# Two unread products of 512 columns ahead of the first transposes of the probabilities in layers 1 and 3

## The chip, the cores and the metric

The kernel runs on one core of one Trainium2 chip. Times are device microseconds of that core. The median of three runs before the change is 2001.88 us (1987.11 to 2002.51). One execution was also profiled: it took 1999.9 us, of which the program's instructions span 1998.0 us.

## The reference

128 boards of 64 squares with 256 features pass through four layers. Each layer adds to x a function of h = relu(layernorm(x)). Layers 0, 1 and 3 are masked attention (8, 4 and 4 heads), layer 2 is a gated graph layer with tanh scores.

```python
def _L1_gnn_ref(x, adjacency_mask, Wq, Wk, Wv, Wo, bo):
    q = split_heads(x @ Wq)
    k = split_heads(x @ Wk)
    v = split_heads(x @ Wv)
    sim = jnp.einsum('bhid,bhjd->bhij', q, k) * scale
    sim = jnp.where(adjacency_mask[:, None, :, :], sim, neg)
    attn = jax.nn.softmax(sim, axis=-1)
    out = jnp.einsum('bhij,bhjd->bhid', attn, v)
    return out @ Wo + bo
...
h = jnp.maximum(_layernorm(x, axis=-1), 0.0)
x = x + _L1_gnn_ref(h, adj, L1_gnn_Wq, ...)
```

Layer 3 is the same function as layer 1 with weights of its own.

## The kernel before

Four boards (256 tokens) make a group, and there are 32 groups. Two groups are worked on at a time, in two slots with buffers and semaphores of their own; 16 passes take all groups. Slot 1 runs half a pass behind slot 0: each engine goes through the same list of steps (`STEPS`) for both slots, merged by a table of numbers (`ORDER`), so on every engine the order of the two slots' steps is fixed and written out. PE's program is unrolled over all 16 passes. Engines meet only through semaphores.

An attention step list for one slot on PE is: `turn` (transposes of the normalised x, L609), `q`, `k`, `v` (the projections, each weight split into a high and a low part of type fp32r), `scores`, then for each half of the heads `pt` (transposes of the probabilities, L683), `heads` (probabilities times v), and at the end `out` (the output projection, tile oT). Every product goes through the helper `mm`, so PE's rows name L483 whatever the step; the tiles tell the steps apart: `kT,qT` is `scores`, `probsT,v` is `heads`, `w_hi,oT` and `w_lo,oT` are `out`, and `consts,probs` are the transposes of `pt`.

Around `pt` the steps hand work to and fro. DVE masks the scores (L1164), takes the row maximum (L1170), ACT takes the exponential (L914), DVE normalises (L1178, L1180). PE's `pt` waits for that (`probs`). ACT copies the transposed probabilities to SBUF (L921), `heads` waits for the copy, ACT and DVE split the result into high and low parts (L924, L989, tile oT), and `out` waits for both parts.

With the lag between the slots, layer 1 of one slot always runs beside layer 3 of the other. So there are two kinds of stretch in a pass. In what is called stretch A here, slot 1 is in layer 1 and slot 0 in layer 3; in stretch B it is the other way round. In A, PE's order is: `v` of layer 3, `pt` 0 of layer 1, `scores` of layer 3, `heads` 0, `pt` 1 and `heads` 1 of layer 1, `out` 0 of layer 1, `pt` 0 of layer 3, `out` 1 of layer 1, `heads` 0, `pt` 1, `heads` 1 and `out` 0 of layer 3, and then layer 2 of slot 1 begins. In B, `pt` 0 of layer 1 stands between the two halves of `v` of layer 3, `scores` of layer 3 stands ahead of the last `heads` of layer 1, and both `out` of layer 1 stand ahead of `pt` 0 of layer 3.

PSUM has four banks of 512 columns for each slot. Bank 3 holds v until ACT has copied it out (`v_sb`, L906); the next steps that write it are `heads` 0 and, later, `out` 1.

Of the kernel before, what the change touches and what calls it, by code (L numbers as in the profile page):

```python
# [29 lines left out]
P = 128  # L30
# [126 lines left out]
def build(nc, x_in, adjq_in, adjt_in, mats_in, cols_in, rows_in, cst_in, out):  # L157
# [8 lines left out]
    with ctx:  # L166
        def sb(name, shape, dt, scope=ctx):
            return scope.enter_context(nc.sbuf_tensor(name, shape, dt))
# [9 lines left out]
        WHI = sb("w_hi", [P, MATS, DC, D], F32R)  # L178
# [91 lines left out]
        def bank(s, n):  # L270
            return PS[:, 4 * s + n, :]
# [42 lines left out]
        def units(a):  # L314


            first, blocks = ((0, 2), (4, 1), (6, 1))[a]
            return [(first + 2 * j + cj, 2 * j + cj, j, cj) for j in range(blocks) for cj in range(2)]

        def turned(a):  # L320

            us = units(a)
            return [us[0:2], us[2:4]] if len(us) == 4 else [us[0:1], us[1:2]]

        def norm_halves(a, v):

            return v.eight[2 * NORM_OF[a]:2 * NORM_OF[a] + 2]
# [56 lines left out]
        def alone(eng):  # L384


            eng.sem_inc(setup["waited"], 1)
# [93 lines left out]
        def _(pe):  # L481
            def mm(o, lhsT, rhs, start, stop):
                return nc.tensor.matmul(o, lhsT, rhs, start=start, stop=stop, skip_group_check=True)  # L483
# [121 lines left out]
            def transposed_h(s, a, t, v):  # L605

                pe.wait_ge(S[s]["xn_ready"], norm_halves(a, v)[t])
                for c in range(DC):
                    last = nc.tensor.transpose(bank(s, H_BANKS[c])[:, t * P:t * P + P],  # L609
                                               XN[s][:, t * D + c * P:t * D + c * P + P], IDENT)  # L610
                    if t == TT - 1:
                        last.then_inc(S[s]["hT_ps"], 1)

            def features_out(s, o, m, oc, halves=None):


                for c in range(DC):
                    if halves:
                        pe.wait_ge(S[s]["hT_hi"], halves[c])
                    mm(o, WHI[:, m, c, oc * P:oc * P + P], HT[s][:, 0, c, :], c == 0, False)  # L620
                    mm(o, WLO[:, m, c, oc * P:oc * P + P], HT[s][:, 0, c, :], False, False)
                for c in range(DC):
                    if halves:
                        pe.wait_ge(S[s]["hT_lo"], halves[c])
                    last = mm(o, WHI[:, m, c, oc * P:oc * P + P], HT[s][:, 1, c, :], False, c == DC - 1)
                return last

            def tokens_out(o, actT, t, m, start=True, ready=(), halves=()):

                at = slice(t * P, t * P + P)
                for c in range(DC):
                    if ready and t == 0:
                        pe.wait_ge(ready[0], halves[c])
                    mm(o, actT(0, c)[:, at], WHI[:, m, c, :], start and c == 0, False)
                    mm(o, actT(0, c)[:, at], WLO[:, m, c, :], False, False)
                for c in range(DC):
                    if ready and t == 0:
                        pe.wait_ge(ready[1], halves[c])  # L640
                    last = mm(o, actT(1, c)[:, at], WHI[:, m, c, :], False, c == DC - 1)
                return last

            def att(s, k, a, i, v):
                sm, L, n = S[s], ATT[a], v.att[a]
                hd = D // L["heads"]
                two = L["heads"] == 8
                if k == "turn":
                    transposed_h(s, a, i, v)
                elif k in ("q", "k"):  # L650
                    b = 1 if k == "q" else 2
                    last = features_out(s, bank(s, b)[:, i * TOK:i * TOK + TOK], L["mats"] + b - 1, i,
                                        norm_halves(a, v) if k == "q" and i == 0 else None)
                    if i == DC - 1:
                        last.then_inc(sm[k + "_ps"], 1)
                elif k == "v":
                    last = tokens_out(bank(s, 3)[:, i * D:i * D + D], lambda j, c: HT[s][:, j, c, :], i, L["mats"] + 2)
                    if i == TT - 1:
                        last.then_inc(sm["v_ps"], 1)
                elif k == "scores":  # L660

                    pe.wait_ge(sm["q_sb"], n)
                    pe.wait_ge(sm["k_sb"], n)
                    alone(pe)
                    if two:

                        pe.wait_ge(sm["v_sb"], n)
                        alone(pe)
                    for b in range(NB):
                        for u, m, _, _ in units(a):  # L670
                            for half, h in enumerate(HEADS_AT[a][m]):
                                r, c = h * hd % P, h * hd // P
                                last = mm(bank(s, m)[SQ * half:SQ * half + SQ, b * SQ:b * SQ + SQ],
                                          Q[s][r:r + hd, c, b * SQ:b * SQ + SQ],
                                          K[s][r:r + hd, c, b * SQ:b * SQ + SQ], True, True)
                            if b == NB - 1:
                                last.then_inc(sm["s_ps"], 1)
                elif k == "pt":

                    for u, _, j, cj in turned(a)[i]:  # L680
                        pe.wait_ge(sm["probs"], v.eight[u])
                        for at in range(cj * TOK, cj * TOK + TOK, P):
                            last = nc.tensor.transpose(bank(s, 1 - i)[:, at:at + P], PR[s][:, j, at:at + P], IDENT)  # L683
                    last.then_inc(sm["pt_ps"], 1)
                elif k == "heads":

                    pe.wait_ge(sm["v_sb"], n)
                    pe.wait_ge(sm["pt_sb"], v.six[2 * a + i])
                    alone(pe)
                    place = {h: (m, half) for m, pair in enumerate(HEADS_AT[a]) for half, h in enumerate(pair)}  # L690
                    for t in range(TT):
                        for h in range(i * L["heads"] // 2, (i + 1) * L["heads"] // 2):
                            m, half = place[h]
                            _, _, j, cj = units(a)[m]
                            r, at = h * hd % P, cj * 256 + t * P + half * SQ
                            for e in range(2):
                                last = mm(bank(s, O_BANKS[i] + e)[r:r + hd, t * SQ:t * SQ + SQ],
                                          V[s][SQ * e:SQ * e + SQ, t, h * hd:h * hd + hd],
                                          PTS[s][SQ * e:SQ * e + SQ, j, at:at + SQ], True, True)
                    last.then_inc(sm["o_ps"], 1)  # L700
                elif k == "out":
                    if i == 0:

                        pe.wait_ge(sm["oT_lo"], v.six[2 * a])
                    tokens_out(bank(s, Y_BANKS[i])[:, 0:D], lambda j, c: OT[s][:, j, c, :], i, L["mats"] + 3,
                               ready=(sm["oT_hi"], sm["oT_lo"]), halves=v.six[2 * a:]).then_inc(sm["y_ps"], 1)
# [106 lines left out]
            def step(s, what, v):  # L813
                k, a, i = what
                if a == L2:
                    l2(s, k, i, v)
                else:
                    att(s, k, a, i, v)
# [481 lines left out]
```

## Time and profile before

| what | before |
|---|---|
| median of the runs | 2001.88 us |
| profiled execution | 1999.9 us |
| its span | 1998.0 us |
| PE busy | 1842.2 us, 92% |
| DVE busy | 1381.1 us, 69% |
| ACT busy | 996.2 us, 50% |
| granted PE clock, mean | 0.966 |

The first rows of the table are times, the others are from the first part of the page. Busy is the union of an engine's instructions; the rest of the span the engine waits or issues. The granted clock is 1.00 at 2.4 GHz and 0.50 at 1.2 GHz, so its mean over a stretch tells which share of that stretch ran at the lower level.

### The profile page before, as it was taken

The page shows a single profiled execution, that of the slowest core. Times are in us where ns is not written, and L with a number is a line of the kernel's source. Part 1 is how long each engine was busy: PE and PEld are TensorE (multiplying, and loading weights), DVE is VectorE, ACT ScalarE, POOL GpSimd, SP SyncE. Part 2 cuts the span into 40 slices and gives each one's busy share as a digit, 9 for nine tenths or more (in the row PEclk, how much of TensorE's full clock was granted, in tenths as well). Part 3 has the DMA queues.
Part 4 walks back from the last instruction along what each step waited for, and adds up shares of the span by engine and source line. Part 5 has one row for each costly group of instructions (what it writes and reads, how often), then busy time and mean ns, then how long its engine had stood idle before and what let it go on. Part 6 is the DMA issues. An engine that isn't in the chain of part 4 may idle for free.

```text
span 1998.0 us, 58204 instructions
## 1 busy us (share of the span) xinstructions
PE 1842.2 (92%) x23623; PEld 1637.1 (82%) x23623; DVE 1381.1 (69%) x3777; ACT 996.2 (50%) x3707; POOL 153.1 (8%) x265
## 2 busy tenths in 40 slices
PE   7999999999999999999999999999999999999997
PEld 6787888887888887888888888888888888888886
DVE  4677677777677776667677667677677766767674
ACT  4545455445455545455445455445455545455452
POOL 0000000000000000000000000000000000000000
PEclk8999999999999999999999999999999989999898
DMA  6000000000000000000000000000000000000000
GB/s 196 1 13 8 13 13 8 12 13 8 13 13 8 12 13 8 13 13 8 12 13 8 13 13 8 12 13 8 13 13 8 11 13 8 13 13 8 12 7 6
DMA packets 36564, 30.62 MB, mean 15 GB/s; under 512 B 11600, under 2 KB 36176, under 8 KB 36368
## 3 DMA queue, kind: packets, MB, share of 16 engines
q1 hardware_dynamic: 36368, 27.48, 4.6%
q8 instruction: 187, 3.06, 0.6%
q14 instruction: 9, 0.07, 0.0%
HBM read 19.08 MB, written 8.39 MB: 14 GB/s over the span
## 4 chain that ended last, share of the span: by engine, by line
PE 75%; DVE 16%; ACT 4%; issue 4%; DMA 0%; DVEq 0%; SPq 0%; POOL 0%; POOLq 0%
PE ps L483 68%; PE ps L609 3%; PE ps L683 3%; DVE small L1091 2%; ACT probs L914 2%; DVE f L1250 1%; DVE f L1248 1%; DVE xn L1103 1%; DVE x L1255 1%; DVE oT L989 1%; DVE small L1097 1%; DVE kT L1150 1%; DVE probs L1164 1%; PE ps L806 1%; DVE probs L1180 1%
## 5 line engine op out<-in xcount | busy, mean ns | idle before, releaser
L483 PE MATMUL ps<-hT,w_hi 128*128 128x256 f32 x2560 | 487.7, 284 | 3.1 <-DVE hT L1117 1.4
L483 PE MATMUL ps<-w_hi,hT 128*128 128x256 f32 (+1 forms) x1536 | 423.8, 344 | 0.0
L483 PEld LDWEIGHTS ps<-hT,w_hi 128*128 128x128 f32 x2560 | 406.7, 190 | 6.7 <-DVE hT L1117 1.8
L914 ACT ACTIVATE probs<-probs,small 128x64 f32<-128x64 f32 x1024 | 342.1, 337 | 93.7 <-DVE small L1170 92.0
L483 PE MATMUL ps<-hT,w_lo 128*128 128x256 f32 x1280 | 332.8, 282 | 0.0
L483 PEld LDWEIGHTS ps<-w_hi,hT 128*128 128x128 f32 x1536 | 267.6, 188 | 42.6 <-DVE wh L1222 11.5
L470 POOL TENSOR_TENSOR small<-small,consts 128x1 f32<-128x1 f32 x256 | 151.1, 590 | 1818.6 <-DVE small L1099 1818.6
L483 PE MATMUL ps<-w_hi,oT 128*128 128x256 f32 x768 | 207.7, 335 | 56.4 <-DVE oT L989 47.5
L483 PE MATMUL ps<-w_lo,hT 128*128 128x256 f32 (+1 forms) x768 | 249.5, 337 | 0.0
L483 PEld LDWEIGHTS ps<-hT,w_lo 128*128 128x128 f32 x1280 | 243.7, 190 | 0.0
L483 PEld LDWEIGHTS ps<-w_hi,oT 128*128 128x128 f32 x768 | 150.0, 215 | 75.3 <-DVE oT L989 64.2
L914 ACT ACTIVATION_READ_ACCUMULATOR probs<-probs,small 128x1 f32 x1024 | 194.2, 190 | 0.0
L889 ACT ACTIVATE hT<-ps 128x256 fp32r<-128x256 f32 x256 | 86.1, 382 | 209.5 <-PE ps L609 209.5
L921 ACT ACTIVATE probsT<-ps 128x256 f32<-128x256 f32 (+1 forms) x192 | 87.7, 457 | 153.4 <-PE ps L683 149.9
L483 PEld LDWEIGHTS ps<-w_lo,hT 128*128 128x128 f32 x768 | 144.6, 188 | 10.7
L483 PE MATMUL ps<-probsT,v 64*64 64x64 f32 (+1 forms) x4096 | 95.7, 235 | 40.7 <-issue 40.7
L1190 DVE TENSOR_TENSOR x<-ps,x 128x256 f32<-128x256 f32 x192 | 81.3, 424 | 74.6 <-PE ps L483 74.3
L1117 DVE SCALAR_TENSOR_TENSOR hT<-ps,hT 128x256 fp32r<-128x256 f32 x256 | 98.0, 419 | 50.1 <-ACT hT L889 48.2
L483 PE MATMUL ps<-w_hi,ct_hi 128*128 128x256 f32 x512 | 127.0, 286 | 4.0 <-DVE ct_lo L1234 2.9
L483 PEld LDWEIGHTS ps<-probsT,v 64*64 64x64 f32 (+1 forms) x4096 | 68.4, 127 | 70.2 <-issue 60.4
L483 PE MATMUL ps<-w_lo,ct_hi 128*128 128x256 f32 x512 | 124.2, 281 | 0.9 <-issue 0.9
L609 PE MATMUL ps<-consts,xn 128*128 128x128 f32 x512 | 94.0, 299 | 31.9 <-DVE xn L1103 31.7
(128 smaller groups left out, 3330.5 us busy)
## 6 DMA issues: line engine op xcount, KB each, us to landing
x_next<-x SPq DMA_DIRECT2D x32, 256.0 KB, 2.6
out<-x SPq DMA_DIRECT2D x32, 256.0 KB, 2.2
raw_lo<-mats SPq DMA_DIRECT2D x6, 1024.0 KB, 10.0
adj<-adjq SPq DMA_DIRECT2D x64, 16.0 KB, 2.0
raw_hi<-mats SPq DMA_DIRECT2D x1, 1024.0 KB, 11.5
adjT<-adjt SPq DMA_DIRECT2D x64, 8.0 KB, 2.3
raw_lo<-mats SPq DMA_DIRECT2D x1, 512.0 KB, 8.2
raw_consts<-board_consts SPq DMA_DIRECT2D x1, 451.5 KB, 3.0
```

Of the source, the lines that this page charges most:

```text
L470: nc.gpsimd.tensor_tensor(RSTD[s][:, i:i + 1], VE[s][:, i:i + 1], HALF, ALU.pow).then_inc(sm["rstd"], 1)
L483: return nc.tensor.matmul(o, lhsT, rhs, start=start, stop=stop, skip_group_check=True)
L609: last = nc.tensor.transpose(bank(s, H_BANKS[c])[:, t * P:t * P + P], XN[s][:, t * D + c * P:t * D + c * P + P], IDENT)
L683: last = nc.tensor.transpose(bank(s, 1 - i)[:, at:at + P], PR[s][:, j, at:at + P], IDENT)
L806: last = nc.tensor.transpose(bank(s, HAT_BANKS[i])[:, t * P:t * P + P], F[s][:, t * D + i * P:t * D + i * P + P], IDENT)
L889: fn(HT[s][:, 0, c, :], bank(s, H_BANKS[c])[:, 0:TOK], ACT.Relu).then_inc(S[s]["hT_hi"], 1)
L914: last = fn(p, p, ACT.Exp, bias=ROWMAX[s][:, row:row + 1], accum_out=ROWSUM[s][:, row:row + 1])
L921: fn(PTS[s][:, j, at], bank(s, 1 - i)[:, at], ACT.Copy).then_inc(sm["pt_sb"], 1)
L989: return tt(o, full, hi.bitcast(F32), ALU.subtract)
L1091: nc.vector.bn_stats(STATS[s][:, t, :], (XP if a == 0 else X)[s][:, t * D:t * D + D]).then_inc(S[s]["bn"], 1)
L1117: stt(HT[s][:, 1, c, :], bank(s, H_BANKS[c])[:, 0:TOK], 0.0, HT[s][:, 0, c, :].bitcast(F32), ALU.max, ALU.subtract).then_inc(S[s]["hT_lo"], 1)
L1190: tt(X[s][:, at], bank(s, Y_BANKS[i])[:, 0:D], X[s][:, at], ALU.add).then_inc(sm["res"], 1)
```

## The change

Ahead of the first transposes of the probabilities (`pt` with i = 0) in layers 1 and 3, PE now waits for `v_sb` and then multiplies a part of the weights by weights, 128 by 128 by 512 columns, twice, into bank 3 of the slot. Nobody reads the result. The steps of the other engines stay as they are. That adds 2 products in each of 2 layers, 2 slots and 16 passes, 64 pairs or 128 products in all.

```diff
                 elif k == "pt":
 
+                    if a > 0 and i == 0:
+
+                        pe.wait_ge(sm["v_sb"], n)
+                        alone(pe)
+                        for _ in range(2):
+                            mm(bank(s, 3), WHI[:, 0, 0, 0:P], WHI[:, 0, :, :].rearrange("p c o -> p (c o)"), True, True)
                     for u, _, j, cj in turned(a)[i]:
                         pe.wait_ge(sm["probs"], v.eight[u])
```

On PE in stretch A of the first pass, the first pair comes in like this (w_hi are weights, hT is h transposed, the number behind a semaphore is the slot):

```order
 L483 MATMUL ps<-w_lo,hT 128x256
 L483 MATMUL ps<-w_hi,hT 128x256 x2
-L683 MATMUL ps<-consts,probs 128x128 [waits probs_1]
-L683 MATMUL ps<-consts,probs 128x128
+L483 MATMUL ps<-w_hi 128x512 [waits v_sb_1]
+L483 MATMUL ps<-w_hi 128x512
+L689 MATMUL ps<-consts,probs 128x128 [waits probs_1]
+L689 MATMUL ps<-consts,probs 128x128
 L483 MATMUL ps<-kT,qT 64x64 [waits q_sb_0,k_sb_0]
 L483 MATMUL ps<-kT,qT 64x64 x15
```

The pair stands between `v` of slot 0 and the transposes of slot 1; the transposes, and the scores of slot 0 behind them, stand two products later.

On PE in stretch A, the second pair comes in behind the first `out` of slot 1:

```order
 L483 MATMUL ps<-w_lo,oT 128x256
 L483 MATMUL ps<-w_hi,oT 128x256 [waits oT_lo_1] x2
-L683 MATMUL ps<-consts,probs 128x128 [waits probs_0]
-L683 MATMUL ps<-consts,probs 128x128
+L483 MATMUL ps<-w_hi 128x512 [waits v_sb_0]
+L483 MATMUL ps<-w_hi 128x512
+L689 MATMUL ps<-consts,probs 128x128 [waits probs_0]
+L689 MATMUL ps<-consts,probs 128x128
 L483 MATMUL ps<-w_hi,oT 128x256
 L483 MATMUL ps<-w_lo,oT 128x256
```

The second `out` of slot 1 moves back with the transposes of slot 0.

On PE in stretch B, the second pair comes in behind both `out` of slot 0:

```order
 L483 MATMUL ps<-w_lo,oT 128x256
 L483 MATMUL ps<-w_hi,oT 128x256 x2
-L683 MATMUL ps<-consts,probs 128x128 [waits probs_1]
-L683 MATMUL ps<-consts,probs 128x128
+L483 MATMUL ps<-w_hi 128x512 [waits v_sb_1]
+L483 MATMUL ps<-w_hi 128x512
+L689 MATMUL ps<-consts,probs 128x128 [waits probs_1]
+L689 MATMUL ps<-consts,probs 128x128
 L483 MATMUL ps<-probsT,v 64x64 [waits v_sb_1,pt_sb_1]
 L483 MATMUL ps<-probsT,v 64x64 x7
```

Here `heads` of slot 1 is next, and moves back too. The transposes are the old ones; their line is L689 in the changed kernel.

## Rows read from the trace of the kernel before

**Rows 1.** Page, parts 1 and 4: busy time, chain that ended last
```profile
PE 1842.2 (92%) x23623; PEld 1637.1 (82%) x23623; DVE 1381.1 (69%) x3777; ACT 996.2 (50%) x3707; POOL 153.1 (8%) x265
...
PE 75%; DVE 16%; ACT 4%; issue 4%; DMA 0%; DVEq 0%; SPq 0%; POOL 0%; POOLq 0%
```

**Rows 2.** Busy time and granted clock (PEclk) of the middle and of single stretches
```profile
core 0: us, PE busy (x) PEld busy (x) DVE busy (x) ACT busy (x) POOL busy (x), PEclk, DMA share, GB/s
125.00:1970.00 1845.00, 1721.41 (x22422) 1532.04 (x22415) 1297.06 (x3568) 932.74 (x3517) 142.73 (x242) 0.97 0.04 11
...
608.80:623.80 15.00, 12.07 (x157) 10.51 (x156) 11.47 (x37) 8.56 (x35) 1.99 (x4) 0.89 0.05 19
...
728.00:743.00 15.00, 12.07 (x167) 10.22 (x165) 12.17 (x40) 8.59 (x35) 2.40 (x4) 1.00 0.06 19
...
910.00:925.00 15.00, 12.28 (x153) 10.53 (x153) 10.70 (x35) 8.63 (x33) 1.44 (x3) 0.77 0.02 5
```

**Rows 3.** Waits of PE: who waited for whom
```profile
engine line waited for: us in total, times, longest us
PE ps L483 <- DVE oT L989: 47.5, 71, 1.3
PE ps L483 <- issue: 41.6, 77, 1.0
...
PE ps L683 <- DVE probs L1180: 3.1, 1, 3.1
```

**Rows 4.** Timeline of PE, stretch A, full clock (start, length, instruction, count, idle before)
```profile
728.32 0.38 PE L683 MATMUL ps<-consts,probs 128*128 128x128 f32 x2
...
731.41 0.39 PE L483 MATMUL ps<-w_hi,oT 128*128 128x256 f32 x1 [0.38 <-DVE oT L989]
...
733.35 0.38 PE L683 MATMUL ps<-consts,probs 128*128 128x128 f32 x2
...
737.11 0.38 PE L483 MATMUL ps<-w_hi,oT 128*128 128x256 f32 x1 [0.93 <-DVE oT L989]
...
743.55 0.36 PE L483 MATMUL ps<-hT,w_hi 128*128 128x256 f32 x1
```

**Rows 5.** Timeline of PE, another stretch A, in which the clock falls
```profile
609.10 0.38 PE L683 MATMUL ps<-consts,probs 128*128 128x128 f32 x2
...
614.12 0.38 PE L683 MATMUL ps<-consts,probs 128*128 128x128 f32 x2
...
625.25 0.36 PE L483 MATMUL ps<-hT,w_hi 128*128 128x256 f32 x1
```

**Rows 6.** Timeline of PE, a stretch B at full clock
```profile
668.56 0.38 PE L683 MATMUL ps<-consts,probs 128*128 128x128 f32 x2
...
684.61 0.36 PE L483 MATMUL ps<-hT,w_hi 128*128 128x256 f32 x1
```

**Rows 7.** Timeline of PE, another stretch B, in which the clock falls
```profile
909.62 0.38 PE L683 MATMUL ps<-consts,probs 128*128 128x128 f32 x2
...
913.71 0.39 PE L483 MATMUL ps<-w_hi,oT 128*128 128x256 f32 x1 [1.27 <-DVE oT L989]
...
915.97 0.63 PE L683 MATMUL ps<-consts,probs 128*128 128x128 f32 x2
...
920.03 0.41 PE L483 MATMUL ps<-w_lo,oT 128*128 128x256 f32 x1
920.24 0.50 PE L483 MATMUL ps<-w_hi,oT 128*128 128x256 f32 x1
...
927.49 0.36 PE L483 MATMUL ps<-hT,w_hi 128*128 128x256 f32 x1
```

**Rows 8.** Timeline of PE: products of 512 columns in layer 2, full clock
```profile
579.58 0.63 PE L483 MATMUL ps<-w_hi,hT 128*128 128x512 f32 x2
580.05 0.40 PE L483 MATMUL ps<-w_lo,hT 128*128 128x512 f32 x1
```

**Rows 9.** Timeline of DVE in the stretch B of Rows 7
```profile
912.12 0.42 DVE L1164 SCALAR_TENSOR_TENSOR probs<-ps,mask_adj 128x256 f32<-128x256 f32 x1 [1.36 <-PE ps L483]
```

## The prediction

> **What bounds the kernel now.** I read the busy times first, then the chain of work that ended last. PE is busy 92% of the span and carries 75% of the chain; DVE has 16%, ACT 4% [rows 1]. So work added to PE costs its full time, unless it falls into a wait. The next view is the list of PE's waits [rows 3]. The reader should look for the place where the pairs go in. The transposes of the probabilities (L683) waited for the softmax once in the whole run, 3.1 us, and that is the last one, at the end of the last pass. At the other 63 places PE comes straight from its previous product. The waits lie elsewhere: in front of `out`, for the split result of `heads` (47.5 us in 71 waits for DVE's oT), and in front of `heads` ("issue", 41.6 us in 77 waits).
>
> Then I read the granted clock. From 125 to 1970 us it is 0.97 on average [rows 2], so 0.03 / 0.5 x 1845 = 111 us run at 1.2 GHz. Cut into stretches of 15 us around A and B, of which 31 can be laid, the clock is 1.00 in ten, 0.89 in thirteen, 0.77 in five and about 0.67 in three; [rows 2] has one of each of the first three kinds. That is 13 x 3.4 + 5 x 6.8 + 3 x 10.2 = 109 us, so nearly all of the half-clock time of the loop lies in A and B, the two places where one slot's layer 1 runs beside the other's layer 3.
>
> **What half clock costs.** The same work is measured at both levels. In A, from the first transposes of layer 1 to the same product of layer 2 takes 743.55 - 728.32 = 15.23 us at full clock [rows 4] and 625.25 - 609.10 = 16.15 us where 3.4 us are at half [rows 5]: 0.92 us more. In B it is 684.61 - 668.56 = 16.05 us [rows 6] against 927.49 - 909.62 = 17.87 us with 6.8 us at half [rows 7]: 1.82 us more. Both are 0.27 us for each microsecond at half clock, since PE waits for much of such a stretch. All 109 to 111 us cost about 30 us. That is the most that this change can give back through the clock.
>
> **What the change adds.** It adds 64 pairs of products of 512 columns, and nothing to another engine. No trace of before has such a product at these places, but layer 2 has the same form: two of them take 580.05 - 579.58 = 0.47 us of PE at full clock [rows 8]. At half clock a product of 256 columns takes 920.24 - 920.03 = 0.21 us [rows 7], so a pair takes 4 x 0.21 = 0.84 us there. From below the bound is nothing, if the pair lies wholly in a wait. I take 0.47, the row of the same form at the clock at which most pairs run: the transposes behind the second pair take 0.38 us in [rows 4] and [rows 5], and 0.63 us in [rows 7] at half clock; 12 of the 63 places are of the latter kind, all of them second pairs.
>
> The added wait for `v_sb` costs nothing. ACT copies v before it takes the exponentials of the same unit, and these stand ahead of the probabilities that the transposes wait for. What would be queued behind it, if it were late, is all of PE.
>
> Now whether a pair lies beside other work. **First pair**: PE goes from `v` to the transposes with no wait [rows 4 to 7], so the transposes start 0.47 us later, and with them the scores of the other slot and `heads`. DVE cannot use the time: in B it stands 1.36 us waiting for just those scores [rows 9]. ACT's copy of the transposes, the masks, the exponentials and the split of oT all follow from the two, so the wait in front of `out` (0.38 us in A, 1.27 us in B) does not shrink but moves back. **Second pair**: it follows `out` with no wait either, and delays transposes, ACT's copy, `heads`, oT and the next `out`. In A the wait of 0.93 us in front of that `out` moves back too, except for a tenth or so that DVE had in hand. After the stretch PE is dense again in layer 2 and has no slack to make the delay good.
>
> Sum: 63 x 0.47 = 29.6 us, and the last pair is free, since PE waits 3.1 us there [rows 3]. The profiled execution took 1999.9 us, 2.0 us under the median of the runs. 1999.9 + 29.6 = 2029.5, so I forecast **2030 us**. At half clock a pair fills time that other work would have spent at half clock, and so I add nothing for the 12 such places; the upper bound is 12 x (0.84 - 0.47) = 4.4 us more.
>
> **What the pairs do to the clock.** In [rows 5] the second pair's place, 614.12, still has transposes of 0.38 us, and the fall comes later, when `heads` and the wait in front of the last `out` have passed. In [rows 7] the clock has fallen by 915.97, after the wait of 1.27 us in front of `out`, and the second pair's place is just behind it. So in neither stretch does a pair stand in the wait that precedes the fall. It stands 2 to 4 us ahead of it, or behind it. A pair makes PE's work denser where it already came without a gap, and leaves the waits as long as they are. I take the half-clock time as unchanged.
>
> The Trainium skill speaks on this: "TensorE: Matmul & The Clock Gate", section "Why this matters for your kernels", asks for no idle gaps of PE over some 3 us between bursts of matmuls. By that rule there is nothing to win here, for no wait of the loop is that long. The trace does not agree that shorter waits are harmless: the longest in front of `out` is 1.3 us [rows 3], and the clock falls behind it [rows 7]. So by the rule the sum stays 2030 us, and by the trace up to 30 us could come back, which makes the first rival.
>
> **The rivals.**
> 1. The pairs hold the clock up. For it: they add work to the very stretches in which it falls, and ten of 31 stretches stay at 1.00 as it is, so the margin is small. Against it: the waits stay. If all half-clock time goes, the time is 2029.5 - 30 = 1999.5 us; if half goes, 2014.5 us. I give 0.22, and the two ends are its range: no change that can be measured.
> 2. The other side: the pairs are swallowed by waits behind them, because DVE, not PE, sets when `out` starts, and the clock is held as well. It decides at the wait in front of `out`: if that shrinks by 0.47 us, the 31 first pairs cost nothing, 14.6 us, and the 16 second pairs of A, in front of a wait of 0.93 us, another 7.5 us. With the clock gain the time is 2029.5 - 14.6 - 7.5 - 30 = 1977 us. DVE's wait for PE [rows 9] speaks against it. I give 0.05.
> 3. More half-clock time. The pairs lengthen the thin stretches, and waits and falls shift against each other. If all ten stretches that are now at 1.00 fell as the others do, this would add 10 x 0.92 to 10 x 1.82, that is 9 to 18 us: 2039 to 2048 us. I give 0.13.
>
> **How the numbers follow.** The forecast has 0.60: 2030 us, with 2020 to 2036 as its own range, from pairs that are in part absorbed and from the 4.4 us at half clock. The range for 8 in 10 leaves out the second rival, the outer third of the first and the far end of the third: 2004 to 2042 us. A measurement of this kernel tells about 1% from no change, here 1982 to 2022 us. Faster than that is the second rival, 0.05. Within it lie the first rival and a small part of the forecast, 0.25. Slower has 0.70.
>
> **What would show it.** In the profile after, a pair should take 0.47 us at full clock, straight behind `v` or `out` and with no wait ahead, and the waits of PE for oT should add up to about the same 47 us. Should these fall by 15 us or more, the second rival holds. The mean granted clock should stay at 0.97 between 125 and 1970 us; at 0.99 or 1.00 the first rival holds, at 0.95 the third. A full-clock stretch A, from the transposes of layer 1 to the product of layer 2, should be 15.23 + 0.47 = 15.7 us, as the first pair lies ahead of its start. What would make the forecast wrong is, above all, how near the stretches are to holding their clock, which the trace of before does not tell.

## The result, and the profile after

| what | before | after |
|---|---|---|
| median of the runs, us | 1998.34 (four runs) | 2028.36 (2020.53 to 2031.36, four runs) |
| ratio after / before | | 1.0153, 95% interval 1.0100 to 1.0207 |
| profiled execution, us | 1999.9 | 2020.53 |
| its span, us | 1998.0 | 2018.6 |
| its mean granted clock | 0.966 | 0.976 |

The change makes the kernel 1.5% slower, 30 us. Of the four executions after, the profiled one is the fastest; the other three took 2026.98, 2029.73 and 2031.36 us at mean granted clocks of 0.970, 0.968 and 0.967.

The first part of the page after:

```profile
PE 1861.8 (92%) x23751; PEld 1646.0 (82%) x23751; DVE 1380.5 (68%) x3777; ACT 997.0 (49%) x3707; POOL 152.1 (8%) x265
...
PE 75%; DVE 15%; ACT 4%; issue 4%; DMA 0%; DVEq 0%; SPq 0%; POOL 0%; POOLq 0%
```

Against [rows 1] PE has 128 instructions and 19.6 us more, and nearly nothing else has moved: PE is still 92% busy and still carries 75% of the chain.

The timeline of PE after, in a stretch A at full clock (start, length, instruction, count, idle before), answers to [rows 4]; w_hi alone, 128x512, is a pair:

```profile
619.47 0.62 PE L483 MATMUL ps<-w_hi 128*128 128x512 f32 x2
619.93 0.38 PE L689 MATMUL ps<-consts,probs 128*128 128x128 f32 x2
...
623.02 0.38 PE L483 MATMUL ps<-w_hi,oT 128*128 128x256 f32 x1 [0.38 <-DVE oT L995]
...
624.95 0.63 PE L483 MATMUL ps<-w_hi 128*128 128x512 f32 x2
625.41 0.38 PE L689 MATMUL ps<-consts,probs 128*128 128x128 f32 x2
...
629.18 0.39 PE L483 MATMUL ps<-w_hi,oT 128*128 128x256 f32 x1 [0.93 <-DVE oT L995]
...
635.59 0.36 PE L483 MATMUL ps<-hT,w_hi 128*128 128x256 f32 x1
```

The reader should see three things. A pair takes 619.93 - 619.47 = 0.46 us, and neither pair has a wait ahead of it. The waits of 0.38 and 0.93 us in front of `out` are as long as before. And the stretch takes 635.59 - 619.93 = 15.66 us against 15.23 us, 0.43 us more for the one pair that lies between these two rows. The list of PE's waits (us in total, times, longest) agrees:

```profile
PE ps L483 <- DVE oT L995: 48.2, 78, 1.3
PE ps L483 <- issue: 44.2, 78, 1.3
...
PE ps L689 <- DVE probs L1186: 2.3, 1, 2.3
```

In [rows 3] these were 47.5, 41.6 and 3.1 us: nothing was swallowed, but for 0.8 us at the very last place. The clock of the profiled execution is another matter. Busy times and granted clock of the loop, of two stretches A and, in the last row, of a stretch B:

```profile
core 0: us, PE busy (x) PEld busy (x) DVE busy (x) ACT busy (x) POOL busy (x), PEclk, DMA share, GB/s
125.00:1970.00 1845.00, 1717.99 (x22284) 1521.40 (x22284) 1286.29 (x3548) 928.27 (x3503) 141.72 (x242) 0.98 0.04 11
619.00:634.00 15.00, 12.06 (x163) 10.03 (x162) 11.36 (x37) 8.73 (x37) 1.83 (x4) 1.00 0.06 19
...
1349.00:1364.00 15.00, 12.30 (x153) 9.96 (x152) 10.62 (x33) 8.11 (x33) 1.49 (x3) 0.89 0.02 5
1043.80:1058.80 15.00, 12.06 (x156) 10.54 (x155) 10.80 (x34) 8.58 (x32) 1.65 (x3) 0.89 0.05 17
```

The loop has 0.98 where it had 0.97 [rows 2]. This view rounds the clock to two digits; the clock records of the two traces, added up over the loop, hold 68 us at half clock in place of 109. In the second stretch A shown (from 1349 us), 3.4 us run at half clock, and its two rows in the timeline are these:

```profile
1349.32 0.38 PE L689 MATMUL ps<-consts,probs 128*128 128x128 f32 x2
...
1366.25 0.36 PE L483 MATMUL ps<-hT,w_hi 128*128 128x256 f32 x1
```

It takes 16.93 us, 1.27 us more than at full clock. Before, the same 3.4 us cost 0.92 us [rows 4, 5]. One stretch against one says little, so here are all thirty stretches that lie whole in the loop, by the clock records and the timelines. Each is timed from the first projection of layer 3 to the first product behind the turn of the next group, and its cost is what it takes beyond the median of its kind that kept the clock:

| | before | after, profiled execution |
|---|---|---|
| A: kept its clock; at half for 3.4 us; for 6.8 us | 4; 11; none | 6; 7; 2 |
| B: kept its clock; at half for 3.4 us; 6.8 us; 10.2 us | 6; 1; 5; 3 | 8; 6; none; 1 |
| half-clock time in A and in B, us | 37.5 and 68.3 | 37.5 and 30.7 |
| what it cost in all, us | 30.3 | 23.9 |
| cost of a microsecond at half clock, us | 0.29 (0.24 to 0.35) | 0.35 (0.27 to 0.44) |

The half-clock time went in B, where the second pair stands just behind the wait after which the clock falls; the last row of busy times is such a stretch, with 0.89 where [rows 2] has 0.77. But each microsecond at half clock cost more. This is one execution of each kernel; no trace shows the others.

### The profile page after: what moved, and what is told of

Same layout as the page of the kernel before. It is cut to its first block, busy times and chain, and to the rows that moved or that the text cites. A ratio compares the mean times of both kernels' runs of the same rounds, so it can differ in the third digit from the quotient of the medians.

```text
span 2018.6 us, 58524 instructions
## 1 busy us (share of the span) xinstructions
PE 1861.8 (92%) x23751; PEld 1646.0 (82%) x23751; DVE 1380.5 (68%) x3777; ACT 997.0 (49%) x3707; POOL 152.1 (8%) x265
## 3 DMA queue, kind: packets, MB, share of 16 engines
HBM read 19.08 MB, written 8.39 MB: 14 GB/s over the span
## 4 chain that ended last, share of the span: by engine, by line
PE 75%; DVE 15%; ACT 4%; issue 4%; DMA 0%; DVEq 0%; SPq 0%; POOL 0%; POOLq 0%
PE ps L483 68%; PE ps L689 3%; PE ps L609 3%; DVE small L1097 2%; ACT probs L920 2%; DVE f L1256 1%; DVE xn L1109 1%; DVE oT L995 1%; DVE f L1254 1%; DVE x L1261 1%; DVE kT L1156 1%; DVE small L1103 1%; ACT probsT L927 1%; DVE probs L1170 1%; PE ps L812 1%
## 5 line engine op out<-in xcount | busy, mean ns | idle before, releaser
L483 PE MATMUL ps<-w_hi,oT 128*128 128x256 f32 x768 | 201.4, 326 | 57.5 <-DVE oT L995 48.2
L483 PEld LDWEIGHTS ps<-w_hi,oT 128*128 128x128 f32 x768 | 144.7, 207 | 76.9 <-DVE oT L995 65.4
```

## The experiments

Two theories were to be told apart. The first: the pairs lie on PE's path and cost their length, and the clock falls because of the waits, in which no pair stands. The second: what counts for the clock is how much work there is in a stretch, wherever it stands, so the pairs do hold it up, and there are only too few of them. The runs of before that went with these kernels have a median of 1995.96 us with the first four (granted clock 0.965 to 0.973) and 1995.76 us with the others (0.957 to 0.973).

| run | products per pass, place | median, us | ratio, 95% interval | granted clock of its runs |
|---|---|---|---|---|
| the change | 8, ahead of `pt` | 2028.36 | 1.0153 (1.0100 to 1.0207) | 0.967 to 0.976 |
| e1_first | 4, ahead of `pt`, layer 1 | 2024.67 | 1.0132 (1.0079 to 1.0185) | 0.952 to 0.969 |
| e2_second | 4, ahead of `pt`, layer 3 | 2018.95 | 1.0122 (1.0094 to 1.0150) | 0.961 to 0.972 |
| e3_four | 16, ahead of `pt` | 2066.57 | 1.0347 (1.0327 to 1.0367) | 0.965 to 0.969 |
| e4_fill | 12, in the waits ahead of `out` | 1970.83 | 0.9865 (0.9845 to 0.9886) | 0.992 to 0.993 |
| e5_moved | 8, in the waits ahead of `out` | 1972.93 | 0.9891 (0.9857 to 0.9926) | 0.988 to 0.993 |
| e6_fill_plus | 12 in the waits, 8 ahead of `pt` | 1998.22 | 1.0002 (0.9978 to 1.0025) | 0.990 to 0.994 |
| e7_fill_l1 | 7, in the waits of layer 1 | 1984.01 | 0.9945 (0.9920 to 0.9971) | 0.979 to 0.984 |
| e8_fillall | 20, in the waits ahead of `out` and `heads` | 1967.30 | 0.9859 (0.9827 to 0.9891) | 0.993 to 0.994 |

**One pair a stretch.** e1_first keeps the pairs of layer 1 alone, e2_second those of layer 3.

```diff
-                    if a > 0 and i == 0:
+                    if a == 1 and i == 0:
```

(and `a == 2`, the index of layer 3, in the other.)

> Only the pairs of layer 1 (the first of each stretch), 32 of them. Theory: each lies on PE's path and costs its own length. The profile after gives it: a stretch A at full clock, from the first projection of layer 3 to the same product of layer 2, takes 20.44 us against 19.54 us before, a stretch B 19.54 against 18.65 us, so 0.90 and 0.89 us for two pairs, 0.45 us a pair. 32 x 0.45 = 14.4 us, and the half-clock time stays as it was (granted clock 0.966 to 0.970): 1.0072 times before, about 2013 us. Rival: the pairs also win back half-clock time, as the profiled execution after shows (0.976): then 5 to 10 us less, 2003 to 2008 us. Rival: first pairs are swallowed by the waits in front of the output projection: about 1998 us, and the waits for oT fall by 14 us.

> Only the pairs of layer 3 (the second of each stretch), 32 of them, the last one in a wait. Theory: 31 x 0.45 = 14 us, half-clock time as before: about 2012 us, as much as the pairs of layer 1, so the two runs add up to the 30 us of both. Rival: the second pairs stand behind the wait after which the clock falls, and can shorten a fall that has begun; then a stretch B with 6.8 us at half clock becomes one with 3.4 us, and the time is 5 to 8 us less, 2004 to 2007 us.

Measured: 2024.67 and 2018.95 us, 28.7 and 23.0 us over before, where 14.4 and 14 were expected. The two add up to 52 us, where the change, with both pairs, costs 30. The pairs' own price is as expected. At full clock a stretch A, from the first projection of layer 3 to the first product of layer 2 behind the turn of the next group, takes 19.55 us before, 19.96 with the first pair alone, 20.02 with the second alone, 20.45 with both; a stretch B, taken to a product about 1.05 us ahead of that one, 18.65, 19.09, 19.08 and 19.53. That is 0.41 to 0.47 us a pair, and it adds up. What does not add up is the clock, and in the two runs it does so in different ways. The four executions of e1_first took 2012.31, 2023.33, 2026.02 and 2034.33 us at granted clocks of 0.969, 0.961, 0.961 and 0.952: the share at half clock went up, and by how much differs from execution to execution by 22 us. In the profiled one, half clock cost 36.7 us in the thirty stretches, against 30.3 before. e2_second, at 0.961 to 0.972, has no larger share at half clock than before (0.965 to 0.973). Its profiled execution has even less of it in the loop, 82 us, and no stretch B with 6.8 us is left, as its rival had it; but a microsecond of it cost 0.35 us, so that it paid 28.7 us and the gain in time did not come. The two rivals of e1_first fell: there was no gain through the clock, and no wait swallowed a pair. With the pairs at 14 us and these costs of half clock, some 6 us of the profiled e1_first and 3 us of the profiled e2_second stay unexplained. The expectation that the half-clock time costs what it did fell in both.

**Twice the work at the same places.**

```diff
-                        for _ in range(2):
+                        for _ in range(4):
```

> Four products in place of two at every place. Theory: cost is linear, 63 x 4 x 0.225 = 57 us over before, at unchanged half-clock time: about 2055 us (ratio 1.0284). Rival, the clock is held by work at these places and two products were only too few: all half-clock time of the two stretches goes (granted clock 0.99 and over), 30 us come back, and the time is about 2025 us, no longer than with two products.

Measured: 2066.57 us, 70.6 over before, and a loop whose clock is, to the second digit, what it was before:

```profile
125.00:1935.00 1810.00, 1690.27 (x21533) 1496.67 (x21533) 1238.09 (x3407) 887.99 (x3354) 136.11 (x233) 0.97 0.04 11
```

So work at these places doesn't hold the clock, in twice the amount either, and the second theory falls for them. It does move the falls, by the clock records: the thirty stretches have 61 us at half clock in A, where they had 37.5, and 41 us in B, where they had 68.3. The cost is 14 us over the linear 57. A stretch B at full clock takes 20.48 us, 1.83 more than before, 0.46 for each two products, so the products themselves are as expected. Half clock accounts for a part of the rest: none of the stretches A kept its clock, and 3.4 us at half clock in a stretch B cost 21.71 - 20.48 = 1.23 us, 0.36 for each microsecond. As an estimate from this, the 102 us cost 37 us, 7 us more than the 30.3 of before; the other 7 us stay open.

**The same products in the waits.** e4_fill takes the pairs out of `pt` and puts products where PE waits, ahead of the first `out` of layers 1 and 3, into a bank of the other slot that nobody reads then.

```diff
+            def fill(s, a, count, v):
+
+                if count and (s, a, v.once) != (0, 1, 1):
+                    for _ in range(count):
+                        mm(bank(1 - s, 3 - a), WHI[:, 0, 0, 0:P], WHI[:, 0, :, :].rearrange("p c o -> p (c o)"), True, True)
...
                 elif k == "out":
                     if i == 0:
+                        if a > 0:
+                            fill(s, a, {(1, 1): 2, (0, 1): 5, (0, 2): 4, (1, 2): 1}[s, a], v)
```

> The products stand in the waits themselves, in front of the first output projection of layers 1 and 3, in a bank of the other slot that nobody reads: two (A, layer 1), five (B, layer 1), four (A, layer 3), one (B, layer 3), about as long as the wait there (0.38, 1.27, 0.93, 0.35 us). None at the old places. Theory: a fall follows a wait of PE, so products in the waits hold the clock at no cost: granted clock 0.99, half-clock time of the stretches gone, 1998 - 30 = about 1968 us, up to 10 us more where a fill is longer than its wait. Rival, where the products stand doesn't matter, only how many there are in a stretch: the clock is as with four products at the old places (whatever that run shows), and the time is 1998 us less that gain. Rival, the fill is in the way: every product costs its 0.225 us, 16 x 12 x 0.225 = 43 us, about 2040 us.

Measured: 1970.83 us, 25 us under before. Its loop, and its waits:

```profile
125.00:1935.00 1810.00, 1723.76 (x22561) 1521.17 (x22560) 1291.61 (x3564) 930.62 (x3512) 143.22 (x242) 1.00 0.04 11
```
```profile
PE ps L483 <- issue: 43.9, 78, 1.3
PE ps L483 <- ACT oT L932: 7.2, 16, 0.5
PE ps L483 <- DVE oT L997: 6.6, 18, 0.4
```

The clock of the loop is 1.00 (its clock records hold no half clock between 125 and 1935 us), and the waits for oT have gone from 47.5 us [rows 3] to 6.6 us, filled with products. In the timeline of PE the wait of a stretch B, 1.27 us in [rows 7], looks like this:

```profile
663.37 0.46 PE L483 MATMUL ps<-probsT,v 64*64 64x64 f32 x16
663.76 1.42 PE L483 MATMUL ps<-w_hi 128*128 128x512 f32 x5
665.11 0.39 PE L483 MATMUL ps<-w_hi,oT 128*128 128x256 f32 x1
```

From `pt` to `out` it takes as long as it did: 665.11 - 661.01 = 4.10 us against 913.71 - 909.62 = 4.09 us [rows 7], by this row of `pt`:

```profile
661.01 0.38 PE L689 MATMUL ps<-consts,probs 128*128 128x128 f32 x2
```

All thirty stretches A and B ran at full clock, at 19.55 and 18.65 us, just as the undisturbed ones before. So the fill costs nothing in them, and of the price of half clock, which the prediction put at 30 us, 25 us came back in the median and 29 us between the profiled spans (1998.0 and 1968.8 us). Both rivals fell.

**The same number, moved.** To rule out that twelve products a pass do what eight can't, e5_moved has the eight of the change in the waits, two at each.

```diff
-                            fill(s, a, {(1, 1): 2, (0, 1): 5, (0, 2): 4, (1, 2): 1}[s, a], v)
+                            fill(s, a, {(1, 1): 2, (0, 1): 2, (0, 2): 2, (1, 2): 2}[s, a], v)
```

> As many products as in the change, two at a time, but in the waits ahead of the first output projection of layers 1 and 3 and not ahead of the transposes. Theory (the place decides): the half-clock time of the stretches goes as with five, two, four and one products there, granted clock 0.99, and the cost is nothing where the wait is longer than 0.45 us and at most 16 x (0.45 - 0.35) = 2 us elsewhere: 1968 to 1974 us, ratio 0.986. Rival (the number in the wait decides): two products leave most of the waits of 1.27 and 0.93 us open, part of the falls stay, clock 0.975 to 0.985, 1978 to 1990 us.

```profile
125.00:1935.00 1810.00, 1711.04 (x22505) 1509.20 (x22505) 1289.96 (x3559) 930.70 (x3508) 143.56 (x242) 1.00 0.04 11
```
```profile
PE ps L483 <- DVE oT L997: 20.0, 49, 0.6
```

Measured: 1972.93 us, with the loop's clock at 1.00 and 20 us of the wait still open. The place decides, not the number: the same products cost 30 us ahead of `pt` and give back 23 us in the waits. A wait need not be filled to its end. The rival, that the number in the wait decides, fell.

**The pairs' price with the clock held.** e6_fill_plus is e4_fill with the change's own pairs besides.

```diff
                 elif k == "pt":
 
+                    if a > 0 and i == 0:
+
+                        pe.wait_ge(sm["v_sb"], n)
+                        alone(pe)
+                        for _ in range(2):
+                            mm(bank(s, 3), WHI[:, 0, 0, 0:P], WHI[:, 0, :, :].rearrange("p c o -> p (c o)"), True, True)
```

> The filled waits and, besides, the pairs of the change at their own places. With the clock held, this prices the pairs without it: theory 63 x 0.45 = 28 us over the 1970.8 us of the filled waits, about 1999 us, granted clock 0.99, a stretch A 19.55 + 0.90 = 20.45 us, a stretch B 18.65 + 0.89 = 19.54 us. Rival (the pairs' price lies partly in half-clock time, as one pair a stretch cost 28 and 23 us in place of 14): less than 20 us over the filled waits.

```profile
125.00:1970.00 1845.00, 1759.94 (x22735) 1549.38 (x22733) 1296.77 (x3569) 933.74 (x3518) 141.66 (x242) 1.00 0.04 11
```
```profile
609.15 0.38 PE L695 MATMUL ps<-consts,probs 128*128 128x128 f32 x2
...
624.82 0.36 PE L483 MATMUL ps<-hT,w_hi 128*128 128x256 f32 x1
```

Measured: 1998.22 us, 27.4 us over e4_fill, or 27.4 / 63 = 0.43 us a pair. The stretch A between the two rows takes 15.67 us, as in the change at full clock. So the pairs alone, with no half-clock time in the thirty stretches, cost 27 us, and the rival fell. A kernel that holds its clock and pays for the pairs is as long as the kernel before, to within the interval (ratio 1.0002).

**Which wait is behind which fall.** e7_fill_l1 fills the waits of layer 1 alone.

```diff
-                            fill(s, a, {(1, 1): 2, (0, 1): 5, (0, 2): 4, (1, 2): 1}[s, a], v)
+                            fill(s, a, {(1, 1): 2, (0, 1): 5, (0, 2): 0, (1, 2): 0}[s, a], v)
```

> Filled waits only ahead of the output projection of layer 1 (two in A, five in B), none in layer 3. Theory (each wait has its own fall): the falls after the first wait of B (granted clock 0.77 and 0.67 there) go, those of A behind the last heads of layer 3 stay, about 12 x 0.93 = 11 us of the 30: about 1981 us, clock 0.98. Rival (the first wait alone decides both): about 1970 us, clock 0.99.

```profile
125.00:1935.00 1810.00, 1704.12 (x22291) 1513.11 (x22291) 1287.42 (x3554) 928.54 (x3506) 143.55 (x242) 0.99 0.04 11
```

Measured: 1984.01 us. Of the profiled execution's stretches A eight kept their clock and seven fell for 3.4 us, as the theory has it; of the stretches B eleven kept it and four fell for 3.4 us, where the theory had none. The falls of 6.8 and 10.2 us in B are gone. The rival, that the first wait decides for both, fell. Each wait has its part, and since e4_fill, which fills layer 3's waits besides, has no fall at all, those of layer 3 have some of the falls of B too. The kernel has no pairs ahead of `pt`, and yet a microsecond at half clock cost 0.34 us here, from 0.25 to 0.38 in single stretches; so a price above 0.27 is not the pairs' own doing.

**The waits ahead of `heads` as well.** e8_fillall adds two products in four waits of 0.52 us.

```diff
                 elif k == "heads":
 
+                    if (s, a, i) in ((1, 1, 1), (0, 2, 1), (1, 2, 0), (1, 2, 1)):
+                        fill(s, a, 2, v)
```

> The filled waits and two more products in each of the waits of 0.52 us ahead of heads (one place in A in layer 1, three in layer 3), where PE waits for ACT's copy of the transposes. Theory: the clock has nothing left to give there, and two products last 0.45 us, inside the wait: 1971 us, same as the filled waits alone. Rival (they are in the way, since the wait of heads ends while they run): up to 62 x 0.2 = 12 us more, about 1983 us.

```profile
PE ps L483 <- issue: 8.4, 12, 1.0
PE ps L483 <- ACT oT L934: 7.2, 16, 0.5
PE ps L483 <- DVE oT L999: 6.5, 17, 0.4
```

Measured: 1967.30 us, 3.5 us under e4_fill; the intervals of the two ratios overlap, so it counts as the same. The wait of 43.9 us ahead of `heads` is down to 8.4 us, and the products in it cost nothing that can be measured. The rival fell. This kernel has the lowest median of the study, by the ratio 1.4% under the kernel before.

## Why the prediction was right, and where it was not

**The price of the pairs** held. 0.47 us was put down for one; the rows after say 0.46, the stretches 0.41 to 0.47, and e6_fill_plus 0.43 with nothing of the clock in it. 63 of them are 27 to 28 us, where the sum had 29.6: this term was 2 us too large.

**The path** held. The waits in front of `out` moved back and did not shrink (0.38 and 0.93 us, 48.2 us in all), so the second rival, that they swallow the pairs, fell. The last pair was free: it took its time out of the wait there, which went from 3.1 to 2.3 us. The stretch A was forecast at 15.7 us and takes 15.66.

**The price of half clock in the kernel before**, 30 us in all, was read rightly: the thirty stretches, timed one by one, add up to 30.3 us, and e4_fill got 25 us of the median back.

**The half-clock time as unchanged** held in the three executions that are not traced, as far as their mean clocks tell: 0.967 to 0.970, near the 0.966 of before. It did not hold in the profiled one. There the loop has 68 us at half clock, not 109, and what went is in B. The prediction gave no weight to a pair that stands just behind the wait. The traces speak against that: B has 31, 34 and 41 us at half clock in the three with a second pair there and open waits (the change, e2_second, e3_four), and 68 and 78 us in the two without a second pair and with open waits (before, e1_first). With one traced execution of each kernel that is likely, but not shown. Nor does the price stay at 0.27 us for a microsecond; it was 0.35. The two work against each other, 23.9 us in place of 30.3. In the thirty stretches the pairs add 15 x (0.90 + 0.88) = 26.7 us, and 26.7 - 6.4 = 20.3 us is what the profiled execution should have been longer by; its span is longer by 20.6 us. The medians give a like sum without a trace. Half clock costs 2028.36 - 1998.22 = 30 us with the pairs; without them it costs 1995.76 - 1970.83 = 25 us by the later runs of before, or 1998.34 - 1970.83 = 28 us by the four that went with the change. So the cost of half clock moved by -6 us in one execution and by some +3 to +5 us in the median, where the prediction had nothing; the two medians of before differ by about as much.

That the forecast of 2030 us lies within 2 us of the median is therefore in part luck: its pairs are 2 us too dear, it starts from an execution of before that is 2 to 4 us over the medians, and it leaves out up to 5 us of half clock that go the other way. Why one pair alone raised the share at half clock, up to a granted clock of 0.952 in one execution, and why a microsecond of it costs 0.24 us in one stretch and 0.44 us in another, the runs do not tell.

**The first rival**, that the pairs hold the clock, had the right price and the wrong place. Products do hold this clock, but in the wait that precedes the fall. The prediction had argued that the pairs stand ahead of that wait or behind it, and not in it; e3_four against e5_moved shows that this is what counts. Sixteen products a pass at the pairs' places leave the loop at 0.97, eight in the waits bring it to 1.00.

The Trainium skill, "TensorE: Matmul & The Clock Gate", section "Why this matters for your kernels", asks for no idle gaps of PE over some 3 us between bursts of matmuls. Keeping to that was not enough here: no wait of PE in the loop is longer than 1.3 us, the clock fell all the same, and filling these waits took the loop from 0.97 to 1.00.

## What to carry to other kernels

In this kernel, work that is put in to keep TensorE's clock up paid where it stands in the wait itself, ahead of the instruction that waits, in a buffer that is free at that moment; there it cost nothing, and filling a part of the wait was enough. About three microseconds ahead of a wait, on a path that is already dense, the same work was paid in full each time it ran. The place of a fall is read from the granted clock over short stretches, and the stretches that kept their clock give the price of those that did not; take that price from many of them, since it differs from one to the next.

## What the runs showed of the hardware that was not expected

The clock fell to 1.2 GHz for 3.4 to 10.2 us at a time behind waits of PE of 0.4 to 1.3 us, in stretches in which PE is still busy for 80% of the time (12.07 of 15 us [rows 2]). The busy time of a stretch does not tell whether its clock held: [rows 2] has two stretches A that are busy for 12.07 of 15 us, one at 1.00 and one at 0.89.

How long the clock stays low is not the same from execution to execution of one program: the mean granted clock of before went from 0.957 to 0.973 over its sixteen later runs, and its time from 2012.10 to 1988.97 us. As an estimate from these two ends, 0.086 and 0.054 of the span, 173 and 107 us, are at half clock, and 23 us over 66 us is 0.35 us for each microsecond of it.
